# Encoder residual ahead of the difference of queries, identity products in the attention with distances and next to the last router, result stored by group

## The reference, cut to what matters

```python
x = x + _L0_xattn_ref(_layernorm(x), ctx_768, ...)
x = x + _L0_attn_ref(_layernorm(x), ...)      # encoder with kernel features
x = x + _L0_ffn_ref(_layernorm(x), ...)       # 8 experts, 2 chosen
x = x + _L1_xattn_ref(_layernorm(x), ctx_768, ...)
x = x + _L1_attn_ref(_layernorm(x), ...)      # 16 heads, distances
x = x + _L1_ffn_ref(_layernorm(x), ...)       # 32 experts, 8 chosen
return x
```

```python
data_dash = jnp.einsum('bnhd,md->bnhm', data * dn, proj)
diag = jnp.sum(jnp.square(data), axis=-1, keepdims=True) * (dn * dn) / 2.0
qf = ratio * (jnp.exp(data_dash - diag - mx) + EPS_KERN)    # mx: maximum over m for queries, over all for keys
num = jnp.einsum('bnhm,bhmd->bnhd', qf, kv)
out1 = _layernorm(x + attn_out, ln1_g, ln1_b)
```

```python
scores = jnp.einsum('bhld,bhsd->bhls', qh, kh) * inv_sqrt_d + bias[None]   # bias = -slope * |l - s|
attn = jax.nn.softmax(scores, axis=-1)
out = jnp.einsum('bhls,bhsd->bhld', attn, vh)
```

```python
logits = flat @ gate_w.T
h = jax.nn.silu(flat @ wg.T) * (flat @ wu.T)
acc + w[:, None] * (h @ wd.T)
```

## Time and profile before

| | |
|---|---|
| median of 3 runs | 2746.99 us (2746.29 to 2753.16) |
| the profiled execution | 2745.56 us, span 2743.6 us |
| mean granted clock of TensorE | 0.956 |
| busy: PE, PEld | 2550.0 us (93%), 2165.7 us (79%) |
| busy: DVE, ACT, POOL | 1647.3 us (60%), 1506.5 us (55%), 1028.4 us (37%) |
| transfers | 132.90 MB, 48 GB/s over the span |

### The profile page before, as it was taken

One profiled execution on the slowest core, in us unless ns is written; L12 is line 12 of the kernel. 1 busy time (PEld: TensorE's weight loads), 2 busy tenths in 40 slices (PEclk: granted clock), 3 DMA queues, 4 the chain that ended last, 5 costly groups with the idle time before them and its releaser, 6 DMA issues. The chain is left out here.

```text
span 2743.6 us, 94744 instructions
## 1 busy us (share of the span) xinstructions
PE 2550.0 (93%) x38959; PEld 2165.7 (79%) x38959; DVE 1647.3 (60%) x3286; ACT 1506.5 (55%) x4047; POOL 1028.4 (37%) x1208
## 2 busy tenths in 40 slices
PE   6999999999988999998589997999999898999998
PEld 5888888888867888876479895777777676999997
DVE  3555555555576666665655545777777565555553
ACT  3555555555466666665544445777777443444443
POOL 2343343343330000003344445666666333344443
PEclk9999999999999999998789998999999796899999
DMA  5322222222161111100100002011010100000001
GB/s 198 125 88 86 86 86 89 95 98 86 37 245 55 38 38 46 38 31 2 56 13 0 0 1 58 23 29 29 23 29 24 51 0 2 1 0 0 0 0 31
DMA packets 41912, 132.90 MB, mean 48 GB/s; under 512 B 5333, under 2 KB 19289, under 8 KB 36953
## 3 DMA queue, kind: packets, MB, share of 16 engines
q1 hardware_dynamic: 41818, 131.56, 14.2%
HBM read 110.58 MB, written 20.97 MB: 48 GB/s over the span
## 5 line engine op out<-in xcount | busy, mean ns | idle before, releaser
L566 POOL TENSOR_TENSOR l_probs<-l_probs,l_rden 128x1024 f32<-128x1024 f32 x128 | 242.4, 1893 | 429.7 <-DVE l_rden L424 429.7
L508 ACT ACTIVATE l_probs<-ps,l_nmax 128x257 f32<-128x257 f32 x512 | 236.3, 474 | 226.2 <-DVE l_nmax L418 226.2
L967 POOL TENSOR_TENSOR l_probs<-l_probs,l_rden 128x1024 f32<-128x1024 f32 x128 | 242.4, 1894 | 171.6 <-DVE l_rden L818 171.6
L418 DVE TENSOR_REDUCE l_nmax<-ps 128x2 f32<-128x514 f32 x256 | 165.4, 687 | 217.4 <-PE ps L303 217.4
L903 ACT ACTIVATE l_probs<-ps,l_nmax 128x257 f32<-128x257 f32 x512 | 236.3, 474 | 59.7 <-DVE l_nmax L812 59.7
L2764 POOL TENSOR_TENSOR m_hh<-m_hh,m_comb_t 128x512 f32<-128x512 f32 (+2 forms) x160 | 143.3, 896 | 224.1 <-DVE m_hh L2690 224.1
L303 PE MATMUL ps<-l_ctxQ,l_q 32*128 32x257 f32 x3072 | 202.6, 392 | 7.1 <-ACT l_probs L508 6.4
L2690 DVE TENSOR_TENSOR m_hh<-ps,m_sg 128x512 f32<-128x512 f32 (+2 forms) x160 | 95.6, 597 | 180.9 <-ACT m_sg L2532 180.7
L812 DVE TENSOR_REDUCE l_nmax<-ps 128x2 f32<-128x514 f32 x256 | 165.5, 688 | 61.2 <-PE ps L704 57.9
L823 DVE COPY l_pT<-ps 128x512 f32<-128x512 f32 x256 | 164.9, 686 | 52.2 <-PE ps L713 48.0
L343 PE MATMUL ps<-l_pT,l_ctxK 128*32 128x128 f32 x6144 | 194.2, 275 | 0.8 <-DVE l_pT L461 0.8
(11 more groups left out here) (372 smaller groups left out, 6734.2 us busy)
## 6 DMA issues: line engine op xcount, KB each, us to landing
l_ctxQ<-in_ctx_q SPq DMA_DIRECT2D x32, 1542.0 KB, 6.5
enc_dash<-kept SPq DMA_DIRECT2D x32, 512.0 KB, 3.3
l_ctxT<-in_ctx_t SPq DMA_DIRECT2D x32, 385.5 KB, 3.3
l_ctxK<-in_ctx_k SPq DMA_DIRECT2D x32, 384.0 KB, 3.1
kept<-enc_va SPq DMA_DIRECT2D x10, 512.0 KB, 3.2
kept<-enc_qsq SPq DMA_DIRECT2D x6, 512.0 KB
kept<-enc_ksq SPq DMA_DIRECT2D x6, 512.0 KB, 2.9
kept<-enc_qfT SPq DMA_DIRECT2D x5, 512.0 KB, 2.9
```

Source lines behind the costliest of these rows:

```text
L418: nc.vector.tensor_reduce(nmax[:, par, 2 * half:2 * half + 2], ps[:, S_B + 2 * half:S_B + 2 * half + 2, 0:NK], AX.X, ALU.max, negate=True) ...
L508: nc.scalar.activation(probs[:, par, hg, :], ps[:, S_B + hg, 0:NK], ACT.Exp, bias=nmax[:, par, hg:hg + 1], accum_out=den[:, par, hg:hg + 1 ...
L566: nc.gpsimd.tensor_tensor(pr, pr, rden[:, b, :, None].to_broadcast([P, HG, NK - 1]), ALU.mult).then_inc(norm_ok, 1)
L967: nc.gpsimd.tensor_tensor(pr, pr, rden[:, b, :, None].to_broadcast([P, HG, K_W]), ALU.mult).then_inc(norm_ok, 1)
```

## The change

Four edits.

1. In the encoder's attention VectorE does the residual of tile t - 1 after the maximum and the sum of the queries, and ahead of their difference.
2. `keep_clock(nc, k, bank, n)` is new: n products of the identity with itself, 128 by 128, into a bank whose content nobody needs. In the attention with distances there are 8 ahead of the first wait, 3 in each of the first three steps, none in step 0, and 2 in each step from 1 on, between the queries' and the value product.
3. The same next to the last router: 8 ahead of the groups, and one at the start of each group.
4. The result goes out inside the last stage, in transfers of four tiles (the last group as three and one), each as soon as `x_ok` says that its tiles are finished. The block of the store is gone.

```diff
-                def exponent_q(t, j):
+                def largest_q(t):
                     dve.wait_ge(dq_mm, t + 1)
                     nc.vector.tensor_reduce(mx[:, :], heads(both(BC)), AX.X, ALU.max).then_inc(mx_ok, 1)
                     dve.wait_ge(mx_ok, t + 1)
                     dve.wait_ge(dq_ok, t + 1)
                     nc.vector.tensor_tensor(cc[:, :], dq[:, :], mx[:, :], ALU.add).then_inc(cc_ok, 1)
+
+                def exponent_q(t, j):
                     dve.wait_ge(cc_ok, t + 1)
                     nc.vector.tensor_tensor(heads(eq[:, j, :]), heads(both(BC)),
...
                 def step(t, j, has, turns):
                     if has(1):
-                        exponent_q(t + 1, 1 - j)
+                        largest_q(t + 1)
                     if has(-1):
                         residual(t - 1, 1 - j)
+                    if has(1):
+                        exponent_q(t + 1, 1 - j)
                     if has(0):
                         softened(t)
...
+def keep_clock(nc, k, bank, n):
+    for _ in range(n):
+        nc.tensor.matmul(k.ps[:, bank, 0:P], k.ident[:, :], k.ident[:, :], start=True, stop=True)
...
                 if has(2):
                     keys_queries(t + 2, j)
+                if has(-1):
+                    keep_clock(nc, k, O_B, 2)
+                elif not has(0):
+                    keep_clock(nc, k, O_B, 3)
+                if has(2):
                     value(t + 2, j)
...
+            keep_clock(nc, k, O_B, 8)
             pe.wait_ge(set_ok, 3)
             run(pe, step)
...
+        @block.sync
+        def _(sp):
+            cuts = list(range(0, T, 4)) + [T - 1, T]
+            by_tile = out_dram.rearrange("(t p) d -> p t d", p=P)
+            for a, b in zip(cuts, cuts[1:]):
+                sp.wait_ge(x_ok, b)
+                sp.dma_start(by_tile[:, a:b, :], k.x[:, a:b, :]).then_inc(stored, 16)
+            sp.wait_ge(stored, 16 * (len(cuts) - 1))
...
+            keep_clock(nc, k, ACC + 1, 8)
             for g in range(NG):
+                keep_clock(nc, k, ACC + 1, 1)
                 if g > 1:
                     pe.wait_ge(xf_ok, g - 1)
...
-            sp.dma_start(out_dram.rearrange("(t p) d -> p t d", p=P), k.x[:, :, :]).then_inc(stored, 16)
-            sp.wait_ge(stored, 16)
```

More of the change, by code:

```diff
@@ L2389, in _, with stage_moe1 @@
             run(pool, step)
-def stage_moe1(nc, k, bufs):
+def stage_moe1(nc, k, bufs, out_dram):
     UNITS, START = [8, 8, 6, 6, 5], [0, 8, 16, 22, 28]
@@ L2424, in stage_moe1 @@
         four = lambda b: ps[:, b, :].rearrange("p (t q) -> p t q", t=4)
+        stored = sem("stored")
         block = ctx.enter_context(nc.Block())
+        @block.sync
[6 more added lines that the diff above has]
+            sp.wait_ge(stored, 16 * (len(cuts) - 1))
         @block.tensor
@@ L2783, in _ @@
             tile(T - 1, 1, last=True)
-def stage_store(nc, k, out_dram):
-    with ExitStack() as ctx:
-        stored = k.sem("stored")
-        block = ctx.enter_context(nc.Block())
-        @block.sync
-        def _(sp):
-            sp.dma_start(out_dram.rearrange("(t p) d -> p t d", p=P), k.x[:, :, :]).then_inc(stored, 16)
-            sp.wait_ge(stored, 16)
 def program(nc, d, out, scratch, kept):
@@ L2813, in program @@
             stage_alibi(nc, k, al, moe, moe_loads)
-            stage_moe1(nc, k, moe)
-        stage_store(nc, k, out)
+            stage_moe1(nc, k, moe, out)
 def layout(v):
```

## The result

Five runs of the changed kernel took 2710.49 to 2725.59 us, median **2715.32 us**; five of the kernel before, on the same chip, 2745.23 to 2753.57, median 2746.99. The ratio is 0.9885, with a 95% interval of [0.9857, 0.9913]: faster by 1.15%, where 1.8% was forecast. The profiled execution took 2710.49 us. Its page begins so; the columns are busy time, share of the span and instructions, then busy tenths in 40 slices.

The account below looks back on a forecast made before the run. It took TensorE's idle time in the encoder attention and its 1.2 GHz clock in the later stages as the bound. 21.5 + 17 + 4 + 7 = 49.5 us saved gave 2697.5 us, range 2685 to 2717.

Parts of the forecast that it names:

- part 2: Attention with distances: identity products keep TensorE's clock high and save 17 us; bounds 21 us saved and 9 us lost.
- part 1: Encoder attention: residual ahead of the difference removes 30 TensorE waits of 0.73 us, saving 21.5 us.
- rival (b): Encoder attention: residual still late or keys' features become the wait, margin 0.1 to 0.25 us; 2708 us, chance 0.1.
- 27% of them would be saved, 21 us: Attention with distances: saving if all 80.8 us at the low clock went at 2.4 GHz, from 1 - 4.24/5.77.
- The 80.8 us: Attention with distances: three stretches at granted 0.50, of 44.0, 19.3 and 17.5 us, counted as 14 steps.
- rival (a): Clock rises only in part, first stretch and router stay low: 33.5 us saved, 2713 us, chance 0.2.
- Part 3: Last router: identity products raise TensorE's clock and save 4 us; bounds 8 us saved and 3.4 us lost.
- 1.6 us: Last router: time of a group at 2.4 GHz, from TensorE's 1.57 and ScalarE's 1.55 us, saving 1.05 us each.
- fall on idle time: Last router: the eight identity products ahead of the groups would run while TensorE is idle.
- the low start of the experts: After the last router: TensorE, done sooner, waits for VectorE's ranking and may begin at the low clock; 2 us deducted.
- Part 4: End of the kernel: storing the result by group leaves one 64 KB transfer after the last addition, saving 7 us.
- 1.7 us: End of the kernel: time of the last 64 KB transfer, 1.5 us fixed and 0.2 us for the data.

Follow-up runs that it names:

- the wide penalty: Changed kernel with the 16 narrow identity products a step that add the penalty replaced by 4 wide ones: 2711.23 us, ratio 0.9868.

## Why the prediction came out as it did

The time lay in the range, 17.8 us above the forecast and 1.7 below the range's upper end; two of the five runs were above it. Of the 17.8, 14.4 are in the profiled execution (2710.5 for 2696.1), and the other 3.4 because the median is 4.8 us above that execution now and was 1.4 above it before. The 14.4 are 7 of part 2, 4 of parts 3 and 4 together and 1 of part 1; most of the rest is the 3.9 of the cross attention, which is chance.

**Part 1, 21.5 us: right.** 20.6 in the pair of profiles, 21.7 alone, 22.7 between the means of all fourteen profiles, 20.2 +- 3.2 from the runs at equal low time. The steps held too: the residual ended 0.12 us before the keys' transposes, of the 0.1 to 0.25 us of margin that rival (b) doubted; the keys' features did not become the wait; nobody missed the later difference.

**Part 2, 17 us: the size was off**, by 7 us in the profiled pair and by 12 on average. Over the five profiles without products and with the narrow penalty (171.55, 165.67, 168.91, 172.84, 161.60) the stage took 168.1 us, over the four with two products a step (161.60, 163.20, 163.84, 163.08) 162.9: 5.2 us. The price of a product at 2.4 GHz and the room for two of them were right (no idle time left, steps of 4.19 us as without them). Cut at the transposes of `al_o` (32 of them), the stage says where it went:

```
us                  start to   first 3     next 24    last 4     rest   stage
                    first      intervals   intervals  intervals
before              16.63      20.56       110.18     20.20      3.98   171.55
after               15.10      19.89       100.46     22.03      4.11   161.60
5 without, mean     16.90      19.78       107.60     19.85      3.98   168.1
4 with, mean        15.21      20.15       101.31     22.15      4.12   162.9
```

The step that failed is "27% of them would be saved, 21 us", with only "a step or two at either end" and "some of it" waiting for code taken off. The 80.8 us at the low clock were divided by 5.77 us as if all were loop steps slowed by the clock. But of the 44.0 us of the first low stretch, which end at 2204, all up to 2195.87 are the start of the stage and its first steps, and the last 17.5 us are steps met for the first time too. There the clock is worth little. From the square root to 2195.87 TensorE had 36 us of low time before and has 10 now, and the start and the first three intervals are 2.2 us shorter, in place of the 9.7 that 27% of 35.9 us make. Two things are in that. In the five kernels without products the first three intervals take 20.3 to 20.6 us with 20 us of low time and 18.9 with 13, so the clock does shorten them, by 0.2 us a microsecond. With products they take 19.9 to 20.4 us with 7 to 14 of low time: the products' own time takes most of it back.

What the clock has to give is in the loop. In the same five kernels its 24 intervals take 100.6 us and 0.29 for each microsecond of low time in them, of which they have 7 to 38; this agrees with the slope that the runs gave. The changed kernel has none there and reached the floor of 24 x 4.19 = 100.6 us. That won 9.7 us of the profiled execution and 6.3 of the mean. The 5.77 us, too, was the shorter of two steps that alternate at the low clock (5.77 and 6.13 us in the second low stretch), which made the gain of a loop step somewhat too small.

At the tail the kernels with products take 2.3 us more on average. That this is the products' own time is not shown: beside the wide penalty the tail took 19.15 us with them, 19.38 in the kernel with none, and 22.75 in the one with products in the loop alone. The had the sign of it: 35.71 us from the first transpose shown to the one at 2195.87, with two of the three longest steps of the stage in them (7.10 and 7.31 us), and only the step behind it was priced.

The loop's clock is also no fixed sum. It held by itself in one profile of the kernel without products (granted 0.98) and fell in others (0.71 in the variant with the wide penalty); with products it held in most and fell to 0.89 in one. This is rival (a)'s pattern, part of the stretches won, and its 2713 us is nearer to the result than the forecast; of its two mechanisms the first stretch did stay partly low, but not because the eight products end too early: the clock was high through them and fell at 2152.8, among the first steps. The price of a low-clock step that the prediction put at 0.65 us for two products is borne out: 6.76 and 6.42 us with them against 6.23 and 5.84 without, in the two kernels with the wide penalty, 0.55 on average. The prediction cited the Trainium skill (TensorE: Matmul & The Clock Gate, Part 1) for a gate whose point of change differs between runs; the runs here agree, with 23 us between the fastest and slowest of the kernel without products, whose mean clocks were 0.964 and 0.948.

**Part 3, 4 us: mis-sized**, 1.4 us at the end of the router and nothing at the end of the stage. The step that failed is the bound of a group by the larger of two engines' sums, "1.6 us". The two buffers of the transposed input tie group n + 2 to group n through four engines; this is read from the timeline, and no run tests it by itself. At the high clock, two groups of the changed kernel:

```profile
2310.78 0.47 PEld L2517 LDWEIGHTS ps<-ident,m_xn 128*128 128x128 f32 x4
...
2311.53 0.59 ACT L2549 COPY m_xf<-ps 128x512 f32<-128x512 f32 x1 [0.19 <-PE ps L2517]
...
2312.18 0.62 POOL L2781 CAST m_xs<-m_xf 128x512 fp32r<-128x512 f32 x1 [0.94 <-ACT m_xf L2549]
...
2312.83 0.69 DVE L2605 TENSOR_TENSOR m_xs<-m_xf,m_xs 128x512 fp32r<-128x512 f32 x1
...
2314.44 0.47 PEld L2517 LDWEIGHTS ps<-ident,m_xn 128*128 128x128 f32 x4
```

Transpose, copy, the high half on GpSimd, the low half on VectorE, the next normalised tiles, and the transposes two groups on start 3.66 us later: 1.83 us a group even here, and 2.09 on average from the first group to the eighth, where before it was 2.31. The prediction's 2.65 us for before was a sum of loads, some of which overlap. So a group saved 0.2 us and not 1.05, and the seven intervals 1.5. Further, the eight products ahead of the groups ran at the low clock, since the stage before had ended so, and took longer than their idle time:

```profile
2301.27 3.92 PEld L1687 LDWEIGHTS ps<-ident 128*128 128x128 f32 x18 [1.36 <-issue]
...
2305.06 0.87 PEld L2517 LDWEIGHTS ps<-ident,m_xn 128*128 128x128 f32 x4
```

The first transpose of the router comes 2.51 us after the square root, before 1.87, where the prediction had these eight "fall on idle time". And the low start of the experts, for which the prediction took off 2 us, did occur: TensorE stood for 2.70 us ahead of the first expert's transposes (before 2.07) and then had the low clock until 2334, for 3.4 us, where before it kept the high one. From these transposes to the end the stage takes 378.3 us, and 376.6 in the kernel without products: the 1.7 us between them eat what the router had won.

**Part 4, 7 us: right.** 2.0 us from the last addition to the end of the span instead of 9.35, 7.4 us less; 6.2 alone by the profile, 5.4 +- 2.8 by the runs. The rest was to be "1.7 us" and is 2.0; the transfer of 64 KB itself landed 1.5 us after its issue. The Trainium skill (DMA: Bandwidth & Descriptors, Anatomy of one DMA) has the fixed cost of about 2.0 us, by which the prediction had 2.2 for the rest, for transfers that GpSimd issues; this one is issued by SyncE, and its 1.5 us from issue to landing are less than that cost alone.

So the total was held by parts 1 and 4, whose terms came from waits and transfers that the trace shows singly, and the two misses are both in the terms that a higher clock was to bring. That the sum still fell into the range is owed to the range's width. None of the kernels tried is shown to be faster than the changed one; the wide penalty with products in the loop alone (0.9848 [0.9826, 0.987]) has the lowest ratio, but its interval overlaps that of 0.9878 [0.9845, 0.991].

## What to carry to other kernels

Before pricing a low clock, split its stretch by what TensorE waits for inside the steps. Time that stands under "issue" in code met for the first time is mostly not the clock's, and products put there cost their own time. In a loop, put in no more of them than the idle time holds. A stage with double buffers can be as slow as the chain that a buffer goes through in two rounds, whatever its busiest engine needs. Where runs differ by more than the part under test, and the part can't change the clock, compare them at equal mean clock before calling it worthless; where it is meant to change the clock, look at the traces stage by stage.

## What the runs showed of the hardware

- A step of some 412 TensorE instructions took 7.16 us on average where it was met for the first time (granted 0.50 to 0.85; 7.12 at 1.00), and 4.19 when repeated at 1.00, with the same work; an instruction packet of 16 KB came about every 4 us then, and none in the repeated steps. By the 64 bytes an instruction of the Trainium skill (Perfetto Trace Analysis, The 4-stage abstract model) such a step would be 26 KB and its fetch 6.6 us at that pace, an estimate. The twelve packets for seven steps agree with the size; the run with 12% fewer instructions did not confirm the time.
- The spread of one program's times goes mostly with TensorE's clock: 58 of 59 runs of the kernel before have spans from 2733.0 to 2761.3 us, which rise with low time at 0.29 us a microsecond (correlation 0.84, so some 70% of their variance); the other one has 2776.9, at a mean clock of 0.943.
- With identity products in a dense loop the clock held more often: the loop had 7 to 38 us of low time in five profiles without them and 0 to 3 in four with them, beside the narrow penalty. They are neither needed for it in each run (granted 0.98 without) nor enough (0.89 with, beside the wide one).
